# A gather buffer's release taken from ScalarE's relu instead of TensorE's sum, in a four-layer graph network

## What is computed

```python
h = x @ enc_node_w + enc_node_b
e = edge_attr @ enc_edge_w + enc_edge_b
# per layer, with z = relu(layernorm(h)) after the first
msg   = relu(z[src] + e) + 1e-7          # 100000 x 64
m     = msg * t
ex    = exp(m - segment_max(m, dst)[dst])
alpha = ex / (segment_sum(ex, dst)[dst] + 1e-16)
agg   = segment_sum(msg * alpha, dst)
out   = relu(layernorm((z + agg) @ w1 + b1)) @ w2 + b2
h     = h + out                          # (first layer: h = out)
```

## Time and profile before

| | |
|---|---|
| time of the kernel before, median of 3 runs | 5297.16 us (5278.94 to 5298.56) |
| the profiled execution: its time | 5282.58 us |
| the profiled execution: its span | 5280.6 us |
| TensorE matmuls busy | 2419.4 us (46%) |
| VectorE busy | 2887.4 us (55%) |
| ScalarE busy | 1842.4 us (35%) |
| GpSimd busy | 3084.4 us (58%) |
| gathers L495 | 3136, mean 952 ns |
| DMA, mean over the span | 96 GB/s |

### The profile page before, as it was taken

One profiled execution on the slowest core, in us unless ns is written; L12 is line 12 of the kernel. 1 busy time (PEld: TensorE's weight loads), 2 busy tenths in 40 slices (PEclk: granted clock), 3 DMA queues, 4 the chain that ended last, 5 costly groups with the idle time before them and its releaser, 6 DMA issues.

```text
span 5280.6 us, 39054 instructions
## 1 busy us (share of the span) xinstructions
PE 2419.4 (46%) x9927; PEld 1638.7 (31%) x9927; DVE 2887.4 (55%) x3862; ACT 1842.4 (35%) x3505; POOL 3084.4 (58%) x3248
## 2 busy tenths in 40 slices
PE   2566666765334444434433444344442443444444
PEld 1344444443322222223222222232232232222223
DVE  3566666666335555555634555555552555555555
ACT  1344443444223333333322333333332333333334
POOL 4666666653466666666355666666625666666661
PEclk8677676777566766666656667666665666666675
DMA  2344443434123333333313333333321333333332
GB/s 56 106 115 118 116 124 112 121 112 130 41 75 102 97 106 96 102 101 98 96 41 83 105 98 100 101 97 104 96 80 46 100 98 102 96 106 99 96 103 67
DMA packets 419248, 506.78 MB, mean 96 GB/s; under 512 B 184319, under 2 KB 190201, under 8 KB 419004
## 3 DMA queue, kind: packets, MB, share of 16 engines
q1 hardware_dynamic: 312398, 393.85, 23.2%
q0 software_dynamic: 103552, 109.52, 10.8%
q10 hardware_dynamic: 3054, 0.71, 0.1%
HBM read 216.36 MB, written 287.39 MB: 95 GB/s over the span
## 4 chain that ended last, share of the span: by engine, by line
another core or an unknown queue 43%; issue 18%; ACT 17%; DVE 11%; PE 10%; DVEq 1%; POOL 1%; ACTq 0%; DMA 0%; SPq 0%; POOLq 0%
PE pT L774 3%; ACT r L576 3%; ACT decay L583 3%; ACT sw_out L591 3%; DVE M L1057 2%; ACT pX L579 2%; PE pA L744 2%; DVE S L1071 2%; ACT u L578 2%; DVE W L1075 1%; DVE pR L1059 1%; DVE pR L1061 1%; PE pX L763 1%; PE pX L758 1%
## 5 line engine op out<-in xcount | busy, mean ns | idle before, releaser
L495 POOL DMA_INDIRECT zsrc<-z_rows,idx_all x3136 | 2986.9, 952 | 1864.3 <-issue 960.3
L774 PE MATMUL pT<-ident,S 128*128 128x128 f32 x1568 | 568.5, 377 | 2156.8 <-issue 1085.7
L1057 DVE TENSOR_TENSOR_SCAN M<-pR,M,u 128x512 f32<-128x512 f32 x392 | 502.3, 1281 | 1624.2 <-ACT u L578 1522.6
L774 PEld LDWEIGHTS pT<-ident,S 128*128 128x128 f32 x1568 | 337.0, 215 | 2229.9 <-issue 2198.4
L576 ACT ACTIVATE r<-pX 128x512 f32<-128x512 f32 x392 | 233.4, 595 | 2176.8 <-remote 1923.2
L1071 DVE TENSOR_TENSOR_SCAN S<-decay,S,pX 128x512 f32<-128x512 f32 x392 | 501.5, 1279 | 491.6 <-issue 369.8
L758 PE MATMUL pX<-e_in,ident 128*128 128x512 f32 x784 | 697.6, 987 | 118.1 <-ACT e_in L570 91.2
L763 PEld LDWEIGHTS pX<-ident,zsrc 128*128 128x128 f32 x3136 | 566.5, 253 | 405.8 <-issue 325.2
L591 ACT ACTIVATE sw_out<-pT 128x512 f32<-128x512 f32 x784 | 439.5, 589 | 713.4 <-issue 381.0
L763 PE MATMUL pX<-ident,zsrc 128*128 128x128 f32 x3136 | 540.5, 330 | 67.2 <-DMA zsrc<-z_rows,idx_all 67.2
L774 PE MATMUL pT<-ident,W 128*128 128x128 f32 x1568 | 541.4, 359 | 0.0
(11 more groups left out here) (175 smaller groups left out, 1968.7 us busy)
## 6 DMA issues: line engine op xcount, KB each, us to landing
sw_rows<-sw_out SPq DMA_DIRECT2D x784, 256.0 KB
e_in<-e_cols SPq DMA_DIRECT2D x300, 256.0 KB
zsrc<-z_rows,idx_all POOLq DMA_INDIRECT x3136
max_cols<-M SPq DMA_DIRECT2D x392, 128.0 KB
attr_in<-in_edge_attr_dram SPq DMA_DIRECT2D x196, 128.0 KB
e_cols<-e_in SPq DMA_DIRECT2D x98, 256.0 KB
z_rows<-z SPq DMA_DIRECT2D x25, 125.0 KB
node_sw<-sw_rows,row_idx POOLq DMA_INDIRECT x100
```

The source lines that it names most:

```text
L495: pool.indirect_dma_start(zsrc[c % RING][:, t4, h, :], None, z_rows, bass.IndirectOffsetOnAxis(idx_all[:, h, t4, c:c + 1].bitcast(U32), 0) ...
L774: last = pe.transpose(pT[b][:, at:at + P], scanned[c % 2][:, t4:CH:SUB], ident[:, :])
L1057: v.tensor_tensor_scan(M[s][:, 1:CH + 1], pR[s][:, :], u[s][:, :], M[s1][:, CH:CH + 1], ALU.add, ALU.max).then_inc(m_done, 1)
```

## The change

GpSimd's wait ahead of the 8 gathers of a chunk names another semaphore. Before, it waited until TensorE had raised `x_mm` for chunk c - 7. Now it waits until ScalarE has raised `r_done` for chunk c - 7. As the relu of a chunk itself waits for `x_mm` of that chunk, the buffer has been read in either case. No instruction is added, removed or moved on any engine, and the waits of ScalarE and SyncE on `x_mm` stay as they are.

```diff
@@ -488,7 +488,8 @@
                 g0 = value(pool, l * NCH)
                 for c in range(NCH):
                     if c >= RING or not first_layer:
-                        pool.wait_ge(x_mm, done(g0 + (c - RING)))
+
+                        pool.wait_ge(r_done, done(g0 + (c - RING)))
                         pool.sem_inc(pool_passed, 1)
                     for h in range(2):
                         for t4 in range(SUB):
```

## The result

The changed kernel takes 5368.47 us (median of 4 runs, 5366.51 to 5376.12) beside 5290.49 us of the kernel before (4 runs, 5278.94 to 5298.56). The ratio is 1.0152, 95% interval 1.0127 to 1.0177: slower by 78 us. The profiled execution has a span of 5363.5 us, 82.9 us more than before.

What follows compares the result with a forecast made beforehand. The bound was taken to be a loop of TensorE's held signal, GpSimd's wake-up and its gather burst. 210 x 0.60 = 126 us on the median of 5297 gave 5423 us, +2.4%, range 5280 to 5475.

Steps and rivals of the forecast that it cites:

- TensorE's signals are held while GpSimd works off a burst, and the loop goes through GpSimd's wake-up: Edge stage: signal, wake-up, gathers, lag, signal form the bounding loop, 23.66 us for two chunks, 12.33 for one in layer 0.
- a held signal comes through a little behind the burst: Relu starts 3.25 us behind GpSimd's last gather in layer 1, 1.68 us behind it in layer 0.
- 0.60 us for a wait that ends idle time: GpSimd's wait for a buffer ends when the relu is over instead of when it starts, 0.60 us later, with nothing hiding it.
- 210 such waits: GpSimd's waits for buffers that end its idle time, 191 + 19 in the profile; at 0.60 us each they cost 126 us.
- the bursts should stay at 16 gathers in layers 1 to 3 and 8 in layer 0: Expected in the changed trace: GpSimd's burst lengths unchanged, with cycles of 24.26 us and 12.93 us.
- far fewer waits than 210, or bursts of another length: Signs in GpSimd's idle-ending waits and gather bursts that would show the forecast to be wrong.
- the weaker form of the faster rival: A burst starting 0.60 us later may let out a stuck signal, tested on layer 1's sum; chance 0.20 with the strong form.
- The second wait of a pair at nothing: Layers 1 to 3: GpSimd's wait for a pair's second chunk passes 5.85 us behind the wake-up, covered by queued gathers, costing nothing.
- the 5.5 us of cover: Layers 1 to 3: the first 8 gathers, still queued when the second relu ends, keep the burst of 16 from tearing.
- the much slower rival: Layers 1 to 3: second wait passed too late, bursts shrink to one chunk, 12.93 us a chunk, 5635 us; chance 0.05.
- The faster rival in its strong form: Signals held only because GpSimd waits for one; loop opens, 695 us less, about 4600 us; chance 0.20 with a weaker form.
- The rival of no change: Signal late for TensorE's own reason, loop not closed through GpSimd, 0.60 us to spare: time stays at 5297; chance 0.11.

Runs made afterwards that it cites:

- u_done: Kernel before (5288.03 us) with GpSimd waiting, in all layers, for ScalarE's u, one activation behind the relu, instead of the sum: 5500.63 us, ratio 1.039.
- before_2: The kernel before, unchanged, run and traced once more: 4342.82 us, beside the kernel before at 4343.12 us.
- only_first: Kernel before (5288.03 us) with GpSimd's wait moved to the relu's signal in layer 0 alone: 5288.28 us, ratio 0.9985.
- only_later: Kernel before (5288.03 us) with GpSimd's wait moved to the relu's signal in layers 1 to 3 alone: 5378.39 us, ratio 1.0155.
- merge_back: Kernel before (5288.03 us) with TensorE signalling a chunk's transposes once, by 2 at the end, instead of twice: 5297.89 us, ratio 1.0011.
- plain_dma: Kernel before (4348.02 us) with each gather replaced by a plain GpSimd DMA of 128 fixed rows: 3414.56 us, ratio 0.7854.
- memsets: Kernel before (4348.02 us) with each gather replaced by two GpSimd memsets, waiting for its own of the chunk before: 3414.78 us, ratio 0.7856.
- half: Kernel before (4348.02 us) with only 4 of a chunk's 8 gathers issued, the other rows staying zero: 3418.92 us, ratio 0.7863.
- pause8: Kernel before (4348.02 us) with GpSimd waiting ahead of each chunk until its own gathers of the chunk before have landed: 5247.99 us, ratio 1.2073.

## Why the prediction was right, point by point

**TensorE's signals are held while GpSimd works off a burst, and the loop goes through GpSimd's wake-up.** The loop is right for the condition in which the times of 5288 us were taken. u_done and the change move the wake-up by 1.38 and 0.63 us, and the cycle follows with 1.43 and 0.69. The contrast is before_2: the same kernel, where no signal was late, has no loop and no gaps, and takes 945 us less (5288.03 - 4343.12). That condition was met, not made by an edit. There, both edits of the wake-up cost nothing. What was only argued before the runs, the cause of the hold, stays open (below). The reading that a held signal comes through a little behind the burst is right for the steady cycles of layers 1 to 3 and not everywhere: in the earlier trace rows, which the prediction used, the relu starts at 104.95, 24 us late, while the gathers go on without a gap (one starts at 104.17 and the next at 105.42).

**0.60 us for a wait that ends idle time.** Measured 0.63 from relu to gather and another 0.06 in the lag.

**210 such waits.** This is the term that was mis-sized. The prediction said that the bursts should stay at 16 gathers in layers 1 to 3 and 8 in layer 0. Layers 1 to 3 did: about 130 waits x 0.60 = 78 us forecast, 83.5 measured. Layer 0 did not: 80 x 0.60 = 48 us forecast, 2.5 us measured (and only_first within 0.5% of no change). So 126 became 78 in the medians and 82.9 in the spans. The prediction had named its own signs of being wrong: far fewer waits than 210, or bursts of another length. In layer 0 both came (36 waits put down to the relu instead of 76 put down to the sum or to "remote", and bursts of 16), and for that layer the forecast was wrong. That the time still came near it is because layer 0 held the smaller part of the sum. The range, 5280 to 5475, was wide enough to take in no change as well, so it alone would prove little.

**Why layer 0 changed its rhythm.** In the earlier trace rows the sum ends at 612.71, 8.77 us into a burst from 603.94, and is held until behind the burst. In the changed kernel it ends at 626.95, 8.24 us into the burst from 618.71, and is answered at once. A wake-up 0.63 us later starts the burst later, so the sum falls earlier in it. It is tempting to read a limit between 8.24 and 8.77 us out of these two places, but the kernel before has others in layer 0 that no such limit fits:

```profile
554.63 0.94 POOL L495 DMA_INDIRECT zsrc<-z_rows,idx_all  x1 [2.30 <-remote]
...
561.79 1.92 PE L763 MATMUL pX<-ident,zsrc 128*128 128x128 f32 x8
...
563.75 0.60 ACT L576 ACTIVATE r<-pX 128x512 f32<-128x512 f32 x1 [3.60 <-issue]
...
738.71 0.94 POOL L495 DMA_INDIRECT zsrc<-z_rows,idx_all  x1 [2.35 <-remote]
...
744.53 1.45 PE L763 MATMUL pX<-ident,zsrc 128*128 128x128 f32 x8
...
750.38 0.60 ACT L576 ACTIVATE r<-pX 128x512 f32<-128x512 f32 x1 [7.07 <-remote]
```

The first sum ends at 563.71, 9.08 us into its burst, and is answered 0.04 us later. The second ends at 745.98, 7.27 us into its burst, and is held for 4.40 us. What is shown is that the rhythm goes with the wake-up: layer 0 has 37, 38 and 40 bursts of 16 in the three kernels whose wake-up there is later (the changed one, only_first, u_done), and 17, 19 and 12 in the three where it isn't (before, only_later, merge_back). Which property of a sum decides whether its signal gets out is not shown. The prompt answer in layer 0 is the weaker form of the faster rival (a burst that starts 0.60 us later may let a signal out that is stuck now), at another place than the one the prediction tested: in layers 1 to 3 the sum is 13.86 us into its burst (1920.06 - 1906.20) and its signal stays held. In layer 0 the prediction priced the wait and did not ask whether the rhythm would stand a later wake-up.

**The second wait of a pair at nothing.** Right. Bursts of 16 stayed (43 or 44 in each of layers 1 to 3 before, 44 after, counted as above), so the 5.5 us of cover was enough, and the much slower rival with it is refuted.

**The faster rival in its strong form** (the hold needs GpSimd's wait for TensorE) is refuted: GpSimd no longer waits for TensorE, and the signal is still 9.11 us late.

**The rival of no change** is refuted for the condition of the first runs, and is what happens in the other: there GpSimd isn't on a loop. The Trainium skill ("Perfetto Trace Analysis", section on the Tensor Engine instruction) lets the signal out when PSUM has acknowledged the bytes, and gives no time for its way to the other engines. By that rule, with nothing held on the way, the relu follows the sum at once. The trace of before_2 agrees, with 0.03 us; that of the changed kernel in its first run disagrees, with 9.11 us. The same program showed both.

## What to carry to other kernels

A wait on a signal of a later engine is free only while the waiting engine has slack at that wait: 0.63 us cost 0.69 us in each cycle where GpSimd was on the loop, and nothing where it had some 55 us to spare. Count such waits per stage, and ask whether the added time can tip the stage into another rhythm; here that took the whole of one stage's cost away. And measure the kernel before again with each comparison: it was 18% faster in later runs, and set against the earlier 5288 us the 3415 us of plain_dma would have read as 35% less, where its own comparison says 21%.

## What was not expected of the hardware

**One kernel, two times.** The kernel before took 5290 and 5288 us in the first two comparisons, and 4343 to 4348 us in the three after them, with no run in between. In the slower ones TensorE's signals are late for all three waiting engines in most cycles: of chunks 5 to 91 in the first trace of the kernel before, every relu of layers 1 to 3 and 67 of 87 in layer 0 start more than 1 us behind their sum (the median of layers 1 to 3 is 8.9 us). In before_2 none is over 0.13 us behind. The difference is not a matter of clock: the stretch of layer 1 has a granted clock of 0.68 in the earlier trace rows and 0.69 in before_2, both between the two levels of 1.2 and 2.4 GHz. The last four of the five comparisons were on chips numbered 2, 1, 13 and again 2, so the number alone does not decide it; whether the same number is the same chip, the runs don't say.

**What holds the signals is open.** It is not a fixed number of TensorE's signals in a burst (merge_back), not a wait of GpSimd for TensorE (the change itself, u_done), and not the time since the burst began alone (the rows of layer 0 above). Whether the indexed gathers are needed for it, or any DMA that GpSimd issues, or any work of GpSimd, was asked by plain_dma, memsets, half and pause8, and they met only the faster condition, where nothing is held. Beside a kernel before of 5288 us they were not run. Nor is it settled that the change would cost the same 1.5% on another chip in the slower condition; what was measured in it (the change, only_later) agrees at 1.0152 and 1.0155.
